# Layer 2 self-attention: weighted sums as four 32-column tiles, values stored and loaded in parts of 112 and 13 rows

## What is computed

```python
def _mha(xk, xv, xq, Wk, Wv, Wq, Wo, bo, masked):
    K = jnp.einsum('bse,hed->bhsd', xk, Wk)
    V = jnp.einsum('bse,hed->bhsd', xv, Wv)
    ...
    att = jax.nn.softmax(scores / jnp.sqrt(jnp.asarray(sk, scores.dtype)), axis=-1)
    out = jnp.einsum('bhqk,bhkd->bhqd', att, V)
    out = out.transpose(0, 2, 1, 3).reshape(out.shape[0], out.shape[2], -1)
    return jax.nn.relu(out @ Wo + bo)
a = _mha(inputs, inputs, inputs, Wk1, Wv1, Wq1, Wo1, bo1, masked=True)
a = _layernorm(inputs + a, g1, b1)
c = _mha(context_seq, context_seq, a, Wk2, Wv2, Wq2, Wo2, bo2, masked=False)
```

## Times and profile before

| | us |
|---|---|
| median of 3 runs | 3301.15 |
| lowest, highest | 3298.35, 3301.16 |
| profiled execution | 3300.37 |
| its span, first to last instruction | 3298.2 |
| TensorE busy | 3033.1 (92%) |
| VectorE busy | 2286.5 (69%) |
| GpSimd busy | 1876.9 (57%) |
| ScalarE busy | 1746.8 (53%) |
| self-attention's batches, first to last key store | 1796.43 to 2099.56 |

### The profile page before, as it was taken

How to read it: one execution, slowest core, us unless ns; L and a number is a source line. 1 busy time by engine, 2 the same in 40 slices (tenths; PEclk the granted TensorE clock), 3 DMA queues, 4 the chain that set the end, 5 groups by cost and what they waited for, 6 DMA issues and landing times. The chain is left out here.

```text
span 3298.2 us, 75517 instructions
## 1 busy us (share of the span) xinstructions
PE 3033.1 (92%) x30694; PEld 2081.6 (63%) x30694; DVE 2286.5 (69%) x4214; ACT 1746.8 (53%) x2876; POOL 1876.9 (57%) x1054
## 2 busy tenths in 40 slices
PE   7978998999999999999988999799999999569969
PEld 5654546777777777777766777555555555336644
DVE  4556557888888888888854444589999997664455
ACT  3534335666666666666644454356666665225545
POOL 0004546777777777777743112178888887224326
PEclk9989998999999999999999999799999999689979
DMA  7741006767777777777632666533333331505500
GB/s 137 142 117 42 1 15 119 148 134 142 139 148 132 143 140 143 135 137 141 141 54 79 242 238 231 176 82 95 95 95 95 95 95 48 94 1 114 122 1 12
DMA packets 607384, 367.76 MB, mean 112 GB/s; under 512 B 462933, under 2 KB 566626, under 8 KB 606786
## 3 DMA queue, kind: packets, MB, share of 16 engines
q1 hardware_dynamic: 607042, 362.96, 48.8%
HBM read 174.41 MB, written 75.24 MB: 76 GB/s over the span
## 5 line engine op out<-in xcount | busy, mean ns | idle before, releaser
L1769 POOL TENSOR_TENSOR L_plo<-L_p,L_phi 128x1500 bf16<-128x1500 f32 x224 | 659.2, 2943 | 268.4 <-DVE L_phi L1852 268.4
L1715 ACT COPY L_ptlo<-L_lt 128x1536 bf16<-128x1536 bf16 x224 | 322.4, 1439 | 379.7 <-PE L_lt L1639 379.7
L2162 ACT ACTIVATE L2b_p<-L2b_score 125x448 f32<-125x448 f32 x768 | 378.8, 541 | 272.5 <-PE L2b_score L2075 271.5
L1653 PE MATMUL L_acc<-L_chi,L_pthi 125*128 125x128 bf16 x2688 | 462.1, 219 | 0.0
L1655 PE MATMUL L_acc<-L_chi,L_ptlo 125*128 125x128 bf16 x2688 | 461.4, 219 | 0.0
L1654 PE MATMUL L_acc<-L_clo,L_pthi 125*128 125x128 bf16 x2688 | 461.2, 219 | 0.0
L1841 DVE TENSOR_SCALAR_CACHE_REDUCE L_p<-L_score,L_cols 128x1500 f32<-128x1500 f32 x224 | 395.0, 1763 | 53.7 <-PE L_score L1631 53.6
L1852 DVE CAST L_phi<-L_p 128x1500 bf16<-128x1500 f32 x224 | 303.2, 1354 | 146.8 <-ACT L_p L1709 144.8
L1709 ACT ACTIVATE L_p<-L_p,L_least 128x1500 f32<-128x1500 f32 x224 | 346.5, 1547 | 67.9 <-DVE L_p L1841 62.8
L2205 POOL TENSOR_TENSOR L2b_psum<-L2b_p 125x896 f32<-125x896 f32 x128 | 266.8, 2085 | 130.2 <-ACT L2b_p L2162 127.9
L2232 DVE TENSOR_REDUCE L2b_max<-L2b_m 112x1 f32<-112x1000 f32 x256 | 300.5, 1194 | 17.2 <-PE L2b_m L2056 9.4
(11 more groups left out here) (658 smaller groups left out, 7029.6 us busy)
## 6 DMA issues: line engine op xcount, KB each, us to landing
L2b_kst<-L_keys SPq DMA_DIRECT2D x96, 375.0 KB, 5.6
L_ct<-L_ct SPq DMA_DIRECT2D x32, 768.0 KB, 6.0
L2a_ct<-L_ct SPq DMA_DIRECT2D x32, 768.0 KB, 14.9
L_ctx<-dram_ctx SPq DMA_DIRECT2D x32, 750.0 KB
L_keys<-L2a_kout SPq DMA_DIRECT2D x32, 750.0 KB, 7.9
L_values<-L2a_vout SPq DMA_DIRECT2D x32, 750.0 KB
L2b_vin<-L_values SPq DMA_DIRECT2D x32, 750.0 KB
L0x_ctx<-dram_ctx SPq DMA_DIRECT2D x32, 672.0 KB
```

Source lines behind the costliest of these rows:

```text
L1653: pe.matmul(acc, w_hi[0:KP, t, :], v_hi[0:KP, t, :], start=(t == 0), stop=False)
L1715: act.copy(pt_lo[g % 2][:, :, :], lt_ps[:, 0:KT * 128].rearrange("p (t q) -> p t q", t=KT)).then_inc(lo_read, 1)
L1769: pool.tensor_tensor(p_lo[g % 2][:, :, 0:KP], probs[g % RP][:, :].rearrange("q (t k) -> q t k", t=KT), p_hi[g % 2][:, :, 0:KP], ALU.subtra ...
L2162: act.activation(probs[t % RP][:, half * 2 * GW:(half + 1) * 2 * GW], score_ps[half][0:KP, 0:2 * GW], ACT.Exp).then_inc(exp_done, 1)
```

## The change

Three things are edited. (1) The value store of a batch becomes two DMAs, of 112 and of 13 rows, and so does the value load of the next stage; the semaphore targets go from 16 to 32. (2) The weighted sums change sides: the values of four heads, 32 columns of `v_all`, are the weights, and the exponentials of four heads, 4 x 56 = 224 columns, are moved through; four such products go to four 32-column tiles of the array, and four more with a matrix of ones give the sums of exponentials. The result stands with the features on the partitions, so that `back` and its copy on ScalarE go. Each of the 128 rows then holds four heads' columns of which one is its own; VectorE's `own_heads` picks it in four steps with the 0/1 columns `L2b_own`, and `divide` normalises straight into `attnT`. `v_now` and GpSimd's `values` go. (3) `output` and its ReLU and addition move from the second batch of a pair to the first of the next pair. The new form is the one that `narrow_heads_attention` has already (lines 2083 to 2107 and 2249 to 2266).

```diff
@@ key_stacks
-        sp.dma_start(v_in[n % RK][:, :, :], v_dram[n].rearrange("k (t d) -> k t d", d=D)
-                     ).then_inc(v_loaded[n % RK], 16)
+        for p0, p1 in ((0, 112), (112, KP)):
+            sp.dma_start(v_in[n % RK][p0:p1, :, :], v_dram[n, p0:p1].rearrange("k (t d) -> k t d", d=D)
+                         ).then_inc(v_loaded[n % RK], 16)
...
@@ self_attention, sync
                     sp.wait_ge(*freed(b, UNITS.index(("values", 2))))
-                    sp.dma_start(v_dram[b], v_out[b % 2][:, :]).then_inc(v_stored[b % 2], 16)
+                    for p0, p1 in ((0, 112), (112, KP)):
+                        sp.dma_start(v_dram[b, p0:p1], v_out[b % 2][p0:p1, :]).then_inc(v_stored[b % 2], 16)
...
@@ self_attention, tensor
-                def weighted(b, k, half):
-                    if half == 0:
-                        pe.wait_ge(t_read, 2 * b + 2)
-                        pe.wait_ge(v_ready, b + 1)
-                        wait(pe, attn_ready, b)
-                    for h in range(8 * half, 8 * half + 8):
-                        m = pe.matmul(a_ps[0:S, h * VW:(h + 1) * VW], pT[k][:, h * S:(h + 1) * S], v_now[k][:, h, :],
-                                      start=True, stop=True)
-                    if half == 1:
-                        m.then_inc(a_done, 1)
-
-                def back(b, k, outputs):
-                    pe.wait_ge(attn_ready, b + 1)
-                    wait(pe, x_read, b)
-                    wait(pe, relu_done, outputs)
-                    pe.transpose(o_ps[:, XC:XC + S], attn[k][:, :], c["ident"][0:S, 0:S]).then_inc(x_done, 1)
+                def weighted(b, k):
+
+                    pe.wait_ge(t_read, 2 * b + 2)
+                    wait(pe, a_read, b)
+                    for g in range(G):
+                        pe.matmul(a_ps[32 * g:32 * g + 32, 0:GW], v_all[:, b, 32 * g:32 * g + 32],
+                                  pT[k][:, g * GW:(g + 1) * GW], start=True, stop=True,
+                                  skip_group_check=True, tile_position=(0, 32 * g))
+                    for g in range(G):
+                        m = pe.matmul(a_ps[32 * g:32 * g + 32, GW:2 * GW], v_one[:, :],
+                                      pT[k][:, g * GW:(g + 1) * GW], start=True, stop=True,
+                                      skip_group_check=True, tile_position=(0, 32 * g))
+                    m.then_inc(a_done, 1)
...
@@ self_attention, scalar
-                def read_back(b, k):
-                    act.wait_ge(x_done, b + 1)
-                    act.copy(attnT[:, k * S:(k + 1) * S], o_ps[:, XC:XC + S]).then_inc(x_read, 1)
-
...
@@ self_attention, vector
+                def own_heads(b):
+
                     dve.wait_ge(a_done, b + 1)
...
+                    acc = a_ps[:, 0:2 * GW].rearrange("r (x h s) -> r x h s", x=2, h=4)
+                    st.link(dve.tensor_scalar(pair[:, :, :], acc[:, :, 0, :], own4[:, 0:1], None, ALU.mult))
+                    for h in (1, 2):
+                        st.link(dve.scalar_tensor_tensor(pair[:, :, :], acc[:, :, h, :], own4[:, h:h + 1], pair[:, :, :],
+                                                         ALU.mult, ALU.add))
+                    dve.scalar_tensor_tensor(pair[:, :, :], acc[:, :, 3, :], own4[:, 3:4], pair[:, :, :],
+                                             ALU.mult, ALU.add).then_inc(a_read, 1)
+
+                def divide(b, k):
+
+                    dve.wait_ge(a_read, b + 1)
+                    st.link(dve.reciprocal(recip[:, :], pair[:, 1, :]))
+                    if k == 0:
+                        wait(dve, o_done, b // 2)
+                    dve.tensor_tensor(attnT[:, k * S:(k + 1) * S], pair[:, 0, :], recip[:, :], ALU.mult
+                                      ).then_inc(heads_ready, 1)
...
                         rest(b, 2)
-                        normalise(b, k)
+                        own_heads(b)
                         rest(b, 4)
+                        divide(b, k)
```

More of the change, by code:

```diff
@@ L2289, in self_attention @@
 def self_attention(nc, c, name, src, scale, bias, causal, a_all, ct, ct_loaded, load_ct, k_dram, v_dram, stored):
-    J = H // 2
-    VW = D // H + 1
+    J, G, GW = H // 2, H // 4, 4 * S
     with Space(nc) as sp_:
         wq, wk, wv, wo = [c[f"{name}_w{k}"] for k in "qkvo"]
-        own, cw = c[f"{name}_own"], c[f"{name}_cw"]
+        own, cw, own4 = c[f"{name}_own"], c[f"{name}_cw"], c["L2b_own"]
         q_all, k_all = sp_.sb(f"{name}_qall", [128, T]), sp_.sb(f"{name}_kall", [128, T])
@@ L2298, in self_attention @@
         q_own = [sp_.sb(f"{name}_qown{k}", [128, HQ]) for k in range(2)]
-        v_now = [sp_.sb(f"{name}_vnow{k}", [S, H, VW]) for k in range(2)]
+        v_one = sp_.sb(f"{name}_vone", [S, 32])
         p_sb = [sp_.sb(f"{name}_p{k}", [2 * S, J, S]) for k in range(2)]
@@ L2302, in self_attention @@
         pT = [sp_.sb(f"{name}_pT{k}", [S, HQ]) for k in range(2)]
-        recip = sp_.sb(f"{name}_recip", [S, H])
-        attn = [sp_.sb(f"{name}_attn{k}", [S, D]) for k in range(2)]
+        pair = sp_.sb(f"{name}_pair", [128, 2, S])
+        recip = sp_.sb(f"{name}_recip", [128, S])
         attnT = sp_.sb(f"{name}_attnT", [128, 2 * S])
@@ L2324, in self_attention @@
         proj_done, q_read, kv_read = sem("proj_done"), sem("q_read"), sem("kv_read")
-        q_ready, v_ready, ones_ready = sem("q_ready"), sem("v_ready"), sem("ones_ready")
+        q_ready, ones_ready = sem("q_ready"), sem("ones_ready")
         s_done, masked, top_done, shifted, exp_done = [
             sem(n) for n in ("s_done", "masked", "top_done", "shifted", "exp_done")]
[L2328 to L2331, removed]
+        t_done, t_read, a_done, a_read, heads_ready, dve_step = [
+            sem(n) for n in ("t_done", "t_read", "a_done", "a_read", "heads_ready", "dve_step")]
+        o_done, relu_done, o_read = [sem(n) for n in ("o_done", "relu_done", "o_read")]
         cw_split = sem("cw_split")
@@ L2452, in body @@
                             scores(b + 2, k, 1)
-                        if k == 1 and not first:
+                        if k == 0 and not first:
                             output(p - 1)
@@ L2459, in body @@
                         prepare(b, 2)
-                        weighted(b, k, 0)
+                        weighted(b, k)
                         prepare(b, 3)
-                        weighted(b, k, 1)
                         prepare(b, 4)
-                        if not (first and k == 0):
-                            back(b - 1, 1 - k, p if k == 1 else p - 1)
                         prepare(b, 5)
@@ L2472, in _ @@
                 pe.wait_ge(cw_split, 2)
+                pe.wait_ge(ones_ready, 1)
                 for k in range(2):
@@ L2478, in _ @@
                 pairs(body)
-                back(B - 1, 1, B // 2 - 1)
                 output(B // 2 - 1)
@@ L2490, in prepared @@
                     act.wait_ge(u_full[f], n + 1)
-                    if j == 0:
-                        wait(act, (k_stored if kind == "keys" else v_stored)[b % 2], 16 * (b // 2))
+                    if j == 0 and kind == "keys":
+                        wait(act, k_stored[b % 2], 16 * (b // 2))
+                    if j == 0 and kind == "values":
+                        wait(act, v_stored[b % 2], 32 * (b // 2))
                     if kind == "keys":
@@ L2527, in body @@
                         prepared(b, 4)
-                        if not (first and k == 0):
-                            read_back(b - 1, 1 - k)
                         prepared(b, 5)
@@ L2554, in queries @@
                                        ALU.mult).then_inc(q_ready, 1)
[L2556 to L2560, removed]
                 c["early"].all_loaded(pool)
@@ L2565, in _ @@
                 queries(1, 1)
[L2566 to L2570, removed]
                 for b in range(2, B):
-                    if b + 1 < B:
-                        queries(b + 1, (b + 1) % 2)
-                    values(b, b % 2)
+                    queries(b, b % 2)
             @block.vector
@@ L2618, in body @@
                             softmax(b + 2, k)
-                        if k == 1 and not first:
+                        if k == 0 and not first:
                             add(p - 1)
                         rest(b, 2)
-                        normalise(b, k)
+                        own_heads(b)
                         rest(b, 4)
+                        divide(b, k)
                 dve.wait_ge(cw_split, 1)
                 dve.tensor_tensor(cw_lo[:, :, :], cw[:, :, :], cw_hi[:, :, :], ALU.subtract).then_inc(cw_split, 1)
-                for k in range(2):
-                    m = dve.memset(v_now[k][:, :, VW - 1:VW], 1.0)
-                m.then_inc(ones_ready, 1)
+                dve.memset(v_one[:, :], 1.0).then_inc(ones_ready, 1)
                 for u, (kind, n) in enumerate(PROJ):
```

18 lines of the change are left out of this document (5 added, 13 removed).

## The result

The changed kernel took 3249.43 us (median of 3 runs, 3247.40 to 3250.59) against 3301.15 before, a ratio of 0.9839 with a 95% interval of 0.9825 to 0.9853: 51.7 us less. The prediction was 3255, with 3240 to 3280 as its range. The profiled execution took 3247.4 us with a span of 3245.6.

The account below looks back on a forecast made before the run. Five DMA engines were taken to bound the self-attention stage; afterwards 31 batches of 8.05 us plus 8 for low clock give 257.6 against 303.1 us, a gain of 45.5, so 3255 us, range 3240 to 3280.

Parts of the forecast that it names:

- What bounded the stage: Self-attention stage before: five DMA engines carry the 125-row value store, 41 packets of 0.240 us, 9.84 us a stalled batch.
- The stores in parts: Value store as 112 and 13 rows: 24 packets on the busiest engine; the wait for stores goes in full.
- The bounds of 5.8 and 7.2 us: DMA time a batch after the change: 24 packets of 0.240 us, or all 2.32 MB at 322 GB/s.
- TensorE's part: TensorE in a stage batch: 2.34 us go, 1.0 come, so 8.73 becomes 7.4 us.
- What is late next: The ScalarE and VectorE chain sets the batch after the change at 8.05 us, own_heads hidden to 0.06 us.
- TensorE's wait ahead of the third key product: Sign of being right: TensorE waits 0.6 us there for VectorE's second subtraction.
- The clock: Pieces of the stage at the lower clock level add 0 to 14 us; 8 taken.
- low clock with 32-column products: Rival: the clock stays low in the stage, 14.8 us a batch, kernel 3456 us; chance 0.04.
- The stores spread: Denies the rival that one engine or memory stays at 8.6 to 9.3 us a batch, 3268 to 3289; chance 0.13.
- memory was not the limit: Denies the rival that memory at 234 GB/s, not five engines, limits: 9.9 us a batch, 3300; chance 0.04.
- Shorter still: Rival: no low clock and a shorter own_heads, 7.95 us a batch, kernel 3244 us; chance 0.10.
- collision with GpSimd: Rival: the softmax's subtraction on VectorE waits for GpSimd's `queries`, 3 to 12 us, up to 3267; chance 0.12.

Follow-up runs that it names:

- stores_only: The kernel before with only its value store cut into two DMAs of 112 and 13 rows; 3271.58 us, ratio 0.9902.
- sums_only: The kernel after with value store and load each one DMA of 125 rows again, keeping the new weighted sums and later `output`; 3299.54 us, ratio 0.9989.
- stores_124: The kernel before with its value store cut into two DMAs of 124 and 1 rows; 3374.38 us, ratio 1.0215.

## Why the prediction was right

- *What bounded the stage.* Right: five DMA engines for 125 rows. stores_only, sums_only and the share of 0.25 in stores_124 show it. That 41 packets of 0.240 us gave the stalled batch was in part luck: the 0.240 is a mean with 1111 packets in it that carry no rows (0.263 without them), and only happens to be what a row costs with five engines at work. It moved nothing in the forecast's sum, since the chain of ScalarE and VectorE, not the DMA engines, sets the batch after the change.
- *The stores in parts.* Right that the wait goes in full, and that the engines stay below the next limit. The bounds of 5.8 and 7.2 us held: 6.8.
- *TensorE's part.* The weighted sums were put at 1.0 us in the place of 2.3 with `back`. In the kernel after the last key product of the second unit starts at 1892.52 and the next unit at 1893.72, which leaves 1.20 - 0.21 = 0.99 us, both changes of tile form included:

```profile
1892.52 0.37 PE L2395 MATMUL L2a_u<-L2a_ct,L2a_cwlo 128*128 128x500 bf16 x1
1892.83 0.58 PE L2427 MATMUL L2a_a<-L2a_pT,L2a_vall 56*32 56x224 f32 x8
1893.23 0.56 PE L2431 MATMUL L2a_a<-L2a_pT,L2a_vone 56*32 56x224 f32 x8
1893.72 0.27 PE L2399 MATMUL L2a_u<-L2a_cwhi,L2a_ct 128*125 128x128 bf16 x1
```

- *What is late next.* Right, and to 0.05 us: the walk through the earlier trace rows gave 4.49, 5.08, 5.81 and 8.05, and the trace has 4.49, 5.08, 5.81 and 8.10. The first three are the old batch's own times, in an order that the change leaves alone; the last is the forecast. It missed by two small things: the third subtraction ended 0.05 us earlier than said (1896.93, +7.95), and the key product came 0.15 us behind it (1897.08) instead of 0.05. `own_heads` took the 1.43 us of the next stage's. TensorE's wait ahead of the third key product was right as well. In the next batch, which has no output product (as the batch of the earlier trace rows), the last value product starts at 1902.24 and would leave the engine 0.06 later, and the key product starts 0.59 us after that (0.6 was said; the profile counts 0.43 from the end of the last column):

```profile
1902.24 0.22 PE L2401 MATMUL L2a_u<-L2a_cwhi,L2a_ct 128*125 128x128 bf16 x1
1902.89 0.39 PE L2393 MATMUL L2a_u<-L2a_ct,L2a_cwhi 128*128 128x500 bf16 x1 [0.43 <-DVE L2a_kout L2598]
```

  In the batch shown further up the output product comes on top and the profile's wait is 0.16 us.
- *The clock.* This term was mis-sized: 8 us were added for pieces at the lower level, and there were none. The step that failed is the choice of 8 "because TensorE still idles in each batch". TensorE idled 14.1 of 303.1 us before and 11.2 of 248.5 after, nearly the same share, at mean clocks of 0.94 and 1.00; so idling in each batch was no reason for low pieces here. In the table above the mean clock is 1.00 in each kernel whose value copy waits for no store, and 0.98, 0.95, 0.94 and 0.82 in those in which it does. stores_only has TensorE's work of before unchanged and 1.00. That the clock followed these waits is shown; what in them makes it fall, their length or their number, is not (sums_only waits more than before and has 0.95).
- *The sum.* 249.6 + 8 = 257.6 us was forecast for 31 batches and 248.5 measured, 9.1 less. Of these 8 are the clock. The other 1.1 come from two errors that partly cancel: 29 batches took 8.09 instead of 8.05 (1.2 us more), and the last two, which have no scores and no softmax, took 6.99 and 6.83 and had been counted in full (2.3 us less). Behind the stage it was 1.4 us less and ahead of it 3.4 more, both within what these parts scatter between kernels. The gain was forecast at 45.5 us and measured at 51.7, with 54.7 in the stage: the kernel's time came within 5.6 us of 3255 where the stage missed by 9.1, and the difference is that scatter, not foresight.
- *The rivals.* No low clock with 32-column products: 1.00. The stores spread, and memory was not the limit. "Shorter still" came half true: no low clock, but 8.09 us and not 7.95. No collision with GpSimd on the softmax's subtraction: its row in the kernel after reads

```profile
L2564 DVE TENSOR_TENSOR L2a_p<-L2a_p,L2a_top x32: 624/626/898, 1787.1 to 2029.9; 112x448 f32<-112x448 f32 x32
```

  with a median of 0.626 us. In the batch shown `queries` ends at 1892.29 (1890.60 + 1.69), 0.04 us before the subtraction starts: it is near. Whether a shift of either would lengthen the subtraction no run here shows.

## What to carry to other kernels

When the share of DMA time settles at a fraction such as 5 of 16 while someone waits for a transfer, look at how the rows of the transfer divide, and cut it so that its large part has a multiple of 16 rows, as 112 here, where 100, 124 and 125 kept somebody waiting. Ask of a change what it is worth under the limit that holds now and under the one that comes next: the weighted sums here brought 2.5 us alone and about 19 more behind the cut store. A batch time that several engines set by turns can be walked from an unstalled batch of the old trace, wait by wait, to a twentieth of a microsecond; then look who is only just hidden.

## What was not expected of the hardware

- The granted clock was 1.00 in the 248.5 us of the stage once no store was waited for, and 0.82 in the 370 us of stores_124, with TensorE busy 89% of it.
- Packets of about 6 KB took 0.263 us on average before and 0.285 when the same bytes moved at 285 GB/s in place of 234. Worked out from the earlier trace rows, it is 0.24 us with five engines at work and 0.30 with all 16: with all at work, a packet takes a quarter longer.
